# Two batch normalisations: powers of two for both in one set, epsilon and pivot scalars on GpSimd, the weights' mean copied by ScalarE

## The chip, the cores and the metric

The kernel runs on one core of a Trainium2 chip. The metric is the device time of one execution in microseconds (us), as the median of several runs. A core has TensorE (PE for matmuls, PEld for weight loads), VectorE (DVE), ScalarE (ACT), GpSimd (POOL) and SyncE (SP), each with an instruction queue of its own; they meet through semaphores.

## The reference

The input is 8 images of 64 channels and 16 x 16 pixels. Four layers follow each other; the change lies in the third and at the joint with the fourth.

```python
# layers 0 and 1: self attention over the 256 pixels of each image, with a shortcut
# layer 2
def batch_norm(x, gamma, beta):
    mean = jnp.mean(x, axis=(0, 2, 3), keepdims=True)
    var = jnp.mean((x - mean) ** 2, axis=(0, 2, 3), keepdims=True)
    return (x - mean) * rsqrt(var + 1e-5) * gamma[None, :, None, None] + beta[None, :, None, None]
def quantize_w1bit(w):
    return jnp.mean(jnp.abs(w)) * jnp.sign(w)
out = relu(batch_norm(x, gamma0, beta0))
out = conv3x3(out, quantize_w1bit(w0))
out = relu(batch_norm(out, gamma1, beta1))
out = conv3x3(out, quantize_w1bit(w1)) + x
# layer 3: whitening of groups of 4 channels: means, 4x4 covariance, Cholesky, solve, 4x4 weights, bias
```

## The kernel before

The 128 partitions hold two halves of the batch (G = 2) with 64 channels each; the free dimension holds four pairs of images (PAIRS, written q = 0 to 3) of 256 pixels. Everything is written out by hand: each engine has one list of instructions, and its order is the order of the code. The stages are: attention layers 0 and 1 (eight iterations of `project`, `scores`, `values`, `mix`), batch normalisation and convolution 0, batch normalisation and convolution 1, and the whitening.

A convolution is 9 taps on a high and a low part of the input (`hi` and `lo`, 16 bit numbers whose sum is the 32 bit activation). `conv_steps` (line 924) issues 41 steps on TensorE: first images 0 and 2, beside them and five steps later images 1 and 3. Image 2's high part is due at step 18, image 3's at 23, image 2's low part at 27 and image 3's at 32. The weights of a tap are the sign of the weight times a power of two (`tap_values`, line 427, on GpSimd); the factor E, the mean of the absolute weights, is left out of convolution 0 and made good in the epsilon of the second normalisation: its statistics get epsilon / E² added.

`power_of_two(n)` (line 1038) makes, from gamma and beta of normalisation n, the power of two near their maximum and the scaled gamma and beta: five VectorE instructions, each of which waits for the one before (`step`). It stands for n = 0 first of all VectorE's work (line 1117), and for n = 1 amid convolution 0 (line 1232).

Between the inputs of convolution 0 and the statistics of its outputs VectorE has this list (lines 1222 to 1242): the low parts of images 0 and 1 (`first_low`); a copy of the weights' means out of PSUM (`emean`); two instructions for E² and its floor (`esq`); high and low part of image 2 (`later_inputs`); the reciprocal `einv`; high and low part of image 3; `power_of_two(1)`; the statistics of image 0 (`conv0_statistics`); epsilon times the reciprocal, and its addition to the statistics (`eps1`, semaphore `eps1_set`); statistics of image 1; the two pivot scalars `nscale` and `nxm` (semaphore `pivot_set`); statistics of images 2 and 3.

TensorE, after convolution 0, waits for `eps1_set` and for three statistics, adds up the two halves of the batch for images 0 to 2 (`combine(1, range(3))`, line 975), then waits for the fourth statistics and does the rest (line 977). VectorE's `bn_aggr` (line 1211) waits for that; the second normalisation and convolution 1 hang on it. The first normalisation has the same sequence in lines 957 to 962 and 1175; ahead of its last statistics VectorE copies the whitening weights (line 1172, semaphore `w3_set`). GpSimd, in this time, does the tap values of convolution 0, the scale and shift of normalisation 0 (lines 447 to 454), the tap values of convolution 1 (line 456), and the scale and shift of normalisation 1. `keep_warm` issues matmuls on constants whose result is not used.

Of the kernel before, what the change touches and what calls it, by code (L numbers as in the profile page):

```python
# [17 lines left out]
U32 = mybir.dt.uint32  # L18
ALU = mybir.AluOpType
# [3 lines left out]
P = 128  # L23
# [3 lines left out]
N = H * W  # L27
# [23 lines left out]
WARM_START = (6, 5, 4)  # L51
E_SQUARE_MIN = 1e-37
FP16_ROOM = 128.0
# [8 lines left out]
K_ID = 0  # L62
K_MH = K_ID + P
K_FIRST = K_MH + 1
K_AVG = K_FIRST
# [15 lines left out]
def constants():  # L81

    part = np.arange(P)
    same_c = part[:, None] % C == part[None, :] % C
    same_g = part[:, None] // C == part[None, :] // C
    k = np.zeros((P, K_COLS), np.float32)
    k[:, K_ID:K_ID + P] = np.eye(P)
    k[:, K_AVG:K_AVG + P] = 0.5 * same_c
    k[:, K_DIF:K_DIF + P] = np.where(same_c, np.where(same_g, 0.5, -0.5), 0)
    k[:, K_REP:K_REP + P] = (part[:, None] % CJ == part[None, :] % CJ) / NTOT  # L90
    k[:, K_ONES:K_ONES + P] = 1.0 / (P * C * TAPS)
    k[:, K_MASKJ:K_MASKJ + C] = part[:, None] % CJ == part[None, :C] % CJ
    k[:, K_HOT:K_HOT + Q] = (part[:, None] % C) // CJ == np.arange(Q)
    k[:, K_EXPO] = -0.5
    k[:, K_EXPO + 1:K_EXPO + Q] = -0.5 * k[:, K_HOT + 1:K_HOT + Q]
    k[:, K_EPSN:K_EPSN + Q * Q] = (BN_EPS * NTOT / G * k[:, K_HOT:K_HOT + Q, None]
                                   * np.eye(Q)).reshape(P, Q * Q)
    k[:, K_MH] = -0.5
    for g in range(G):
        k[:, K_OWN + g * P:K_OWN + (g + 1) * P] = same_c * (part[:, None] // C == g)  # L100
    return k
# [16 lines left out]
def build(nc, x, attn_w, params, consts, select, conv_w, out):  # L118
    with ExitStack() as ctx:
        def sb(name, shape, dt=F32):  # L120
            return ctx.enter_context(nc.sbuf_tensor(name, shape, dt))
# [35 lines left out]
        bn_b = [sb(f"bn_b{n}", [P, 1]) for n in range(2)]  # L157
        bn_t = [sb(f"bn_t{n}", [P, 8]) for n in range(2)]

        sign = [sb(f"sign{n}", [P, TAPS, C]) for n in range(2)]  # L160
        taps = [sb(f"taps{n}", [P, TAPS, C], BF16) for n in range(2)]
        wabs = [sb(f"wabs{n}", [P, 1]) for n in range(2)]
        esq, einv, eps1 = (sb(name, [P, 1]) for name in ("esq", "einv", "eps1"))
        emean = sb("emean", [P, 2])
# [76 lines left out]
        sign_out, taps_out = sem("sign_out"), sem("taps_out")  # L241
        wabs_out, e_mm = sem("wabs_out"), sem("e_mm")
        bn_v, pivot_set = sem("bn_v"), sem("pivot_set")
        tap_mm, tap_sum_out = sem("tap_mm"), sem("tap_sum_out")
# [108 lines left out]
        def _(pool):  # L353
# [73 lines left out]
            def tap_values(n):  # L427

                pool.wait_ge(sign_out, n + 1)
                pool.wait_ge(pow2_out, n + 1)  # L430
                nc.gpsimd.tensor_scalar(taps[n][:], sign[n][:], bn_t[n][:, 2:3], 1.0,
                                        ALU.mult, ALU.mult).then_inc(taps_out, 1)
                pool.wait_ge(taps_out, n + 1)
# [9 lines left out]
            pool.wait_ge(shift_out, 8)  # L443
            tap_values(0)
            for n in range(2):

                pool.wait_ge(var_out, n + 1)
                pool.wait_ge(rstd_out, n + 1)
                nc.gpsimd.tensor_tensor(bn_s[n][:], bn_t[n][:, 4:5], rstd[n][:], ALU.mult).then_inc(scale_out, 1)
                pool.wait_ge(scale_out, n + 1)  # L450
                nc.gpsimd.tensor_tensor(bn_b[n][:], mv[n][:, 0:1], bn_s[n][:], ALU.mult).then_inc(shift_part, 1)
                pool.wait_ge(shift_part, n + 1)
                nc.gpsimd.tensor_tensor(bn_b[n][:], bn_t[n][:, 5:6], bn_b[n][:], ALU.subtract).then_inc(shift0_set, 1)
                pool.wait_ge(shift0_set, n + 1)
                if n == 0:
                    tap_values(1)
            pool.wait_ge(pre_out, 1)
# [20 lines left out]
        def _(act):  # L478
# [117 lines left out]
            for n in range(2):  # L596
# [8 lines left out]
                for q in range(2):  # L605

                    act.wait_ge(z_out, 2 * n + q + 1)
                    out_hi = hi[n][:, q].rearrange("p r w -> p (r w)")
                    if n == 1 and q == 1:
                        nc.scalar.activation(out_hi, zn[n][:, q], ACT.Relu, scale=rstd[n][:], bias=bn_t[n][:, 5:6],  # L610
                                             accum_out=act_sum[:]).then_inc(hi_act, 1)
                    else:
                        nc.scalar.activation(out_hi, zn[n][:, q], ACT.Relu, scale=rstd[n][:],  # L613
                                             bias=bn_t[n][:, 5:6]).then_inc(hi_act, 1)
                act.wait_ge(shift0_set, n + 1)
                for q in range(2, PAIRS):
                    if n == 1:

                        act.wait_ge(lo_out, q + 1)
                    src = xs[LAYERS][:, quarter(q)] if n == 0 else pb_conv[0][q][:, 0:N]  # L620
                    nc.scalar.activation(act32[:, quarter(q)], src, ACT.Relu, scale=bn_s[n][:],
                                         bias=bn_b[n][:]).then_inc(act_out, 1)

            act.wait_ge(pivot_mm, 1)
# [401 lines left out]
        def _(dve):  # L1026
# [10 lines left out]

            def power_of_two(n):

                t, col = bn_t[n], (P_BNG0, P_BNG1)[n]  # L1040
                step(ve.tensor_reduce(t[:, 0:1], prm[:, col:col + 2], AX.X, ALU.max, apply_absolute_value=True))
                step(ve.tensor_scalar(t[:, 1:2], t[:, 0:1], 1e-30, 1.0 / FP16_ROOM, ALU.max, ALU.mult))
                step(ve.tensor_scalar(t[:, 2:3].bitcast(U32), t[:, 1:2].bitcast(U32), 0x7F800000, None,
                                      ALU.bitwise_and))
                ve.reciprocal(t[:, 3:4], t[:, 2:3]).then_inc(pow2_out, 1)
                dve.wait_ge(pow2_out, n + 1)
                step(ve.tensor_scalar(t[:, 4:6], prm[:, col:col + 2], t[:, 3:4], None, ALU.mult))

# [57 lines left out]
            def statistics(b):  # L1106
# [4 lines left out]
                if b == 0:  # L1111
# [4 lines left out]

            power_of_two(0)
            first_parts(0)
# [47 lines left out]
            statistics(1)  # L1166
            weight_sum(1)
            values_out(7)
            add_shortcut(6)
            statistics(2)  # L1170

            ve.tensor_copy(tt[:, :, Q:2 * Q],
                           prm[:, P_W3:P_W3 + Q * Q].rearrange("p (i r) -> p i r", i=Q)).then_inc(w3_set, 1)
            dve.wait_ge(pv_mm, ITERS)
# [9 lines left out]
            def first_line(n, q):  # L1184

                ve.tensor_scalar(act32[:, quarter(q)], zn[n][:, q], rstd[n][:], bn_t[n][:, 5:6],  # L1186
                                 ALU.mult, ALU.add).then_inc(line_out, 1)
# [21 lines left out]
            for n in range(2):  # L1209
                dve.wait_ge(comb_mm, n + 1)  # L1210
                ve.bn_aggr(mv[n][:], both[:, :, 0:GROUPS]).then_inc(var_out, 1)  # L1211
                dve.wait_ge(var_out, n + 1)
                t = bn_t[n]
                for q in range(2):
                    src = xs[LAYERS][:, quarter(q)] if n == 0 else pb_conv[0][q][:, 0:N]
                    ve.tensor_scalar(zn[n][:, q], src, mv[n][:, 0:1], t[:, 4:5], ALU.subtract,  # L1216
                                     ALU.mult).then_inc(z_out, 1)
# [3 lines left out]
                if n == 0:  # L1221
                    first_line(0, 1)
                    first_low(0, 0)
                    first_low(0, 1)
                    dve.wait_ge(e_mm, 1)
                    step(ve.tensor_copy(emean[:], pb_mean[:, 0:2]))
                    step(ve.tensor_tensor(esq[:], emean[:, 0:1], emean[:, 0:1], ALU.mult))
                    step(ve.tensor_scalar(esq[:], esq[:], E_SQUARE_MIN, None, ALU.max))
                    later_inputs(0, 2)
                    step(ve.reciprocal(einv[:], esq[:]))  # L1230
                    later_inputs(0, 3)
                    power_of_two(1)
                    conv0_statistics(0)
                    step(ve.tensor_scalar(eps1[:], einv[:], BN_EPS * PAIRS * N, None, ALU.mult))
                    dve.wait_ge(stats_out, 1)
                    ve.tensor_tensor(stats[1][:, M2:M2 + 1], stats[1][:, M2:M2 + 1], eps1[:],
                                     ALU.add).then_inc(eps1_set, 1)
                    conv0_statistics(1)
                    ve.tensor_scalar(nscale[:], emean[:, 1:2], -1.0 / N, None, ALU.mult).then_inc(pivot_set, 1)
                    ve.tensor_scalar(nxm[:], mv[0][:, 0:1], -1.0, None, ALU.mult).then_inc(pivot_set, 1)  # L1240
                    conv0_statistics(2)
                    conv0_statistics(3)
                else:
# [3 lines left out]
                    for q in range(2, PAIRS):  # L1247
                        later_inputs(1, q)
            for q in range(PAIRS):
                dve.wait_ge(conv_mm, PAIRS + q + 1)  # L1250
# [132 lines left out]
```

## Time and profile before

| | |
|---|---|
| time, median of 3 runs | 68.54 us (68.48 to 69.81) |
| span of the profiled execution, first to last instruction | 68.0 us |
| median less span, taken as what lies around the span | 0.54 us |
| busy: PE, VectorE, ScalarE, GpSimd | 87%, 70%, 63%, 29% |
| granted TensorE clock, mean | 0.999 |

No time of the profiled execution itself is recorded beside its span, so the median stands for it. In the rows below, a time is microseconds from the start of the span; a duration is that of the instruction, and the next one of the same engine can start before it is over. "xN" puts N like instructions that follow each other in one row. In brackets stands how long the engine was idle before, and what ended the wait; "issue" means that the profile shows nothing it waited for.

### The profile page before, as it was taken

To read this page: it belongs to the slowest core of one execution; us is meant where nothing else is said; L and a number is where in the kernel's file an instruction comes from. 1 tells how busy PE (TensorE), PEld (TensorE's weight loads), DVE (VectorE), ACT (ScalarE), POOL (GpSimd) and SP (SyncE) were. 2 spreads that over 40 slices of the span, in tenths; PEclk is the share of its full clock that TensorE was granted. 3 is DMA by queue.
4 is the path that set the end of the run, shared out by engine and by line. 5 is a ranking of instruction groups with operands and counts; after the bars stand their busy time and mean duration, and the time that the engine had idled before them with its cause. 6 is when DMAs were issued, how large, how long until landed. Compare 5 with 4: busy or idle time off the path is not lost. (4 is left out here: it accounts for less than half of the span.)

```text
span 68.0 us, 2165 instructions
## 1 busy us (share of the span) xinstructions
PE 59.0 (87%) x811; PEld 36.5 (54%) x811; DVE 47.9 (70%) x133; ACT 42.5 (63%) x137; POOL 20.0 (29%) x58
## 2 busy tenths in 40 slices
PE   5969999888989998995999897999769999999910
PEld 3315354446655554652436384598655997955500
DVE  0077569878694989997693856998979978576530
ACT  0710229899999599969999495670018573267630
POOL 5000770733083632766032104200403050036000
PEclk9999999999999999999999999999999999999999
DMA  0878940000000000000000000000000000000044
GB/s 0 236 219 222 339 195 0 0 0 10 0 0 0 5 0 0 0 10 10 0 0 0 0 10 0 0 0 10 0 0 0 10 0 10 0 0 0 0 162 146
DMA packets 2457, 2.71 MB, mean 40 GB/s; under 512 B 400, under 2 KB 2064, under 8 KB 2448
## 3 DMA queue, kind: packets, MB, share of 16 engines
q1 hardware_dynamic: 2160, 2.39, 11.3%
q10 hardware_dynamic: 288, 0.20, 0.9%
q8 instruction: 6, 0.10, 0.6%
q14 instruction: 3, 0.02, 0.1%
HBM read 2.06 MB, written 0.52 MB: 38 GB/s over the span
## 5 line engine op out<-in xcount | busy, mean ns | idle before, releaser
L686 PE MATMUL bank<-const-bfloat16-1.0 128*64 128x512 bf16 x64 | 9.2, 429 | 0.8 <-PEq L1368 0.8
L530 ACT ACTIVATE probs<-bank 128x512 f32<-128x512 f32 x16 | 8.8, 601 | 1.1 <-PE bank L769 1.1
L510 ACT ACTIVATE bank<-bank,negmax 128x256 f32<-128x256 f32 x20 | 9.1, 460 | 0.2 <-DVE negmax L1060 0.2
L808 PE MATMUL both<-probs,vt 128*64 128x256 f32 x56 | 7.6, 387 | 0.3 <-issue 0.3
L1060 DVE TENSOR_REDUCE negmax<-bank 128x2 f32<-128x512 f32 x10 | 6.7, 685 | 1.4 <-PE bank L745 0.8
L510 ACT ACTIVATE both<-both,negmax 128x256 f32<-128x256 f32 x12 | 5.4, 451 | 2.6 <-DVE negmax L1060 2.6
L363 POOL TENSOR_TENSOR cut<-cut 64x256 f32<-64x256 f32 x7 | 4.3, 611 | 8.7 <-DVE cut L1070 5.7
L916 PE MATMUL bank<-hi,taps 64*64 64x225 f16 (+2 forms) x126 | 6.3, 267 | 0.1
L916 PE MATMUL bank<-lo,taps 64*64 64x225 f16 (+2 forms) x126 | 6.2, 266 | 0.0
L686 PEld LDWEIGHTS bank<-const-bfloat16-1.0 128*64 128x64 bf16 x64 | 3.7, 119 | 3.7 <-issue 1.6
L916 PEld LDWEIGHTS bank<-hi,taps 64*64 64x64 bf16 x126 | 5.2, 107 | 0.8 <-issue 0.4
L916 PEld LDWEIGHTS bank<-lo,taps 64*64 64x64 bf16 x126 | 5.6, 107 | 0.0
L1087 DVE CAST qk<-bank 128x512 bf16<-128x512 f32 x7 | 4.8, 683 | 0.5 <-PE bank L713 0.5
L379 POOL TENSOR_TENSOR shift<-negmax,lntot 128x4 f32<-128x4 f32 x8 | 1.6, 203 | 11.9 <-issue 10.5
L808 PEld LDWEIGHTS both<-probs,vt 128*64 128x64 f32 x56 | 4.4, 136 | 1.4 <-issue 0.8
L1060 DVE TENSOR_REDUCE negmax<-both 128x2 f32<-128x512 f32 x6 | 4.1, 683 | 1.1 <-PE bank L745 1.1
L697 PE MATMUL both<-x,aw 128*64 128x256 f32 x24 | 4.8, 484 | 0.1
L370 POOL TENSOR_TENSOR cut<-cut 32x256 f32<-32x256 f32 x7 | 4.3, 611 | 0.5
L510 ACT ACTIVATION_READ_ACCUMULATOR bank<-bank,negmax 128x1 f32 x20 | 4.4, 219 | 0.0
L1093 DVE COPY vt<-bank 128x256 f32<-128x256 f32 x8 | 3.4, 421 | 1.4 <-PE bank L729 1.4
L713 PE MATMUL bank<-cut,half 128*64 128x256 bf16 x32 | 3.8, 315 | 0.3 <-POOL cut L370 0.2
L538 ACT ACTIVATE shift_t<-bank 128x256 bf16<-128x256 f32 x8 | 3.1, 385 | 1.3 <-PE bank L784 1.2
(155 smaller groups left out, 124.8 us busy)
## 6 DMA issues: line engine op xcount, KB each, us to landing
cw<-conv_w SPq DMA_DIRECT2D x2, 288.0 KB, 4.4
x<-x_in SPq DMA_DIRECT2D x4, 128.0 KB, 3.1
out<-res SPq DMA_DIRECT2D x4, 128.0 KB, 1.8
kst<-consts SPq DMA_DIRECT2D x1, 428.0 KB, 5.0
aw<-attn_w ACTq DMA_DIRECT2D x1, 128.0 KB, 2.5
aw<-attn_w SPq DMA_DIRECT2D x1, 128.0 KB, 2.9
half<-select SPq DMA_DIRECT2D x1, 96.0 KB, 3.3
kst<-consts SPq DMA_DIRECT2D x1, 64.5 KB, 4.0
```

Source lines behind the costliest of these rows:

```text
L363: nc.gpsimd.tensor_tensor(some, some, tops(some), ALU.subtract).then_inc(part1_out, 1)
L370: nc.gpsimd.tensor_tensor(some, some, tops(some), ALU.subtract).then_inc(part2_out, 1)
L510: nc.scalar.activation(part, part, ACT.Exp, bias=negmax[:, i % 2, n:n + 1], accum_out=total[:, i % 2, n:n + 1]).then_inc(total_out, 1)
L530: nc.scalar.activation(probs[:, i % 2, g], pb_t[g][:].rearrange("p (t n) -> p t n", t=CH), ACT.Exp).then_inc(exp_out, 1)
L686: mm(bank[lanes(h)], filler[:, lanes(h)], filled, start=True, stop=True)
L697: last = mm(proj(i)[lanes(h)], aw[:, w + h * C:w + (h + 1) * C], x_of(i), start=True, stop=True)
L713: last = mm(to, half[:, 1 + o, lanes(h)], tops(cut[:, i]), start=True, stop=True)
L808: last = mm(mixed(i)[g * C:(g + 1) * C], vt[:, i % 2, t, g * C:(g + 1) * C], probs[:, i % 2, g, t, :], start=(t == 0 and i < ITERS - 1), s ...
L916: last = mm(img(pb_conv[n][q][lanes(to), 0:N])[:, kept(dy, H), kept(dx, W)], taps[n][lanes(g), tap, :], (hi, lo)[part][n][lanes(g), q, shi ...
L1060: ve.tensor_reduce(negmax[:, i % 2, g * CH:(g + 1) * CH], pb_s[(2 * i + g) % 3][:].rearrange("p (t n) -> p t n", t=CH), AX.X, ALU.max, neg ...
L1087: ve.tensor_copy(qk[:, i].rearrange("p o n -> p (o n)"), pb_rep[:]).then_inc(qk_out, 1)
L1093: ve.tensor_copy(vt[:, i % 2], pb_v[:, 0:CH * P].rearrange("p (t c) -> p t c", t=CH)).then_inc(v_out, 1)
```

## The change

- The two sets of five VectorE instructions become one set for both normalisations at the start of the kernel, with twice as many numbers in each. Its last instruction is a `tensor_tensor` with a repeated operand in place of a `tensor_scalar`.
- The copy of the weights' means goes to ScalarE, behind its two last activations for convolution 0. VectorE waits for it (`emean_out`) before the residual of convolution 1.
- The floor, 1 / E², epsilon and its addition to the statistics, and the two pivot scalars go to GpSimd (`epsilon`), behind the scale and shift of normalisation 0. The square and the reciprocal become one power (`ALU.pow` with the exponent -2 from a column of the constants that held another number).
- GpSimd makes the tap values of convolution 1 directly behind those of convolution 0.
- VectorE copies the whitening weights ahead of the last `values_out` rather than ahead of the last statistics.

```diff
-K_MH = K_ID + P
+K_M2 = K_ID + P
...
-    k[:, K_MH] = -0.5
+    k[:, K_M2] = -2.0
...
-                pool.wait_ge(pow2_out, n + 1)
-                nc.gpsimd.tensor_scalar(taps[n][:], sign[n][:], bn_t[n][:, 2:3], 1.0,
+                pool.wait_ge(pow2_out, 1)
+                nc.gpsimd.tensor_scalar(taps[n][:], sign[n][:], pow2[:, n:n + 1], 1.0,
...
             tap_values(0)
+            tap_values(1)
+
+            def epsilon():
+
+                pool.wait_ge(emean_out, 1)
+                nc.gpsimd.tensor_scalar(e_floor[:], emean[:, 0:1], E_MIN, 1.0, ALU.max, ALU.mult).then_inc(floor_out, 1)
+                pool.wait_ge(floor_out, 1)
+                nc.gpsimd.tensor_tensor(einv[:], e_floor[:], kst[:, K_M2:K_M2 + 1], ALU.pow).then_inc(einv_out, 1)
+                pool.wait_ge(einv_out, 1)
+                nc.gpsimd.tensor_scalar(eps1[:], einv[:], BN_EPS * PAIRS * N, 1.0, ALU.mult, ALU.mult).then_inc(eps_out, 1)
+                pool.wait_ge(eps_out, 1)
+                pool.wait_ge(stats_out, 1)
+                nc.gpsimd.tensor_tensor(stats[1][:, M2:M2 + 1], stats[1][:, M2:M2 + 1], eps1[:],
+                                        ALU.add).then_inc(eps1_set, 1)
+                nc.gpsimd.tensor_scalar(nscale[:], emean[:, 1:2], -1.0 / N, 1.0, ALU.mult, ALU.mult).then_inc(pivot_set, 1)
+                nc.gpsimd.tensor_scalar(nxm[:], mv[0][:, 0:1], -1.0, 1.0, ALU.mult, ALU.mult).then_inc(pivot_set, 1)
+                pool.wait_ge(eps1_set, 1)
+                pool.wait_ge(pivot_set, 2)
+
             for n in range(2):
...
-                nc.gpsimd.tensor_tensor(bn_s[n][:], bn_t[n][:, 4:5], rstd[n][:], ALU.mult).then_inc(scale_out, 1)
+                nc.gpsimd.tensor_tensor(bn_s[n][:], gb[:, n, 0:1], rstd[n][:], ALU.mult).then_inc(scale_out, 1)
...
                 if n == 0:
-                    tap_values(1)
+                    epsilon()
...
+                if n == 0:
+                    act.wait_ge(e_mm, 1)
+                    nc.scalar.activation(emean[:], pb_mean[:, 0:2], ACT.Identity).then_inc(emean_out, 1)
...
-            def power_of_two(n):
-
-                t, col = bn_t[n], (P_BNG0, P_BNG1)[n]
-                step(ve.tensor_reduce(t[:, 0:1], prm[:, col:col + 2], AX.X, ALU.max, apply_absolute_value=True))
-                step(ve.tensor_scalar(t[:, 1:2], t[:, 0:1], 1e-30, 1.0 / FP16_ROOM, ALU.max, ALU.mult))
-                step(ve.tensor_scalar(t[:, 2:3].bitcast(U32), t[:, 1:2].bitcast(U32), 0x7F800000, None,
+            def powers_of_two():
+
+                both_gb = prm[:, P_BNG0:P_BNG0 + 4].rearrange("p (n k) -> p n k", n=2)
+                step(ve.tensor_reduce(gb_max[:], both_gb, AX.X, ALU.max, apply_absolute_value=True))
+                step(ve.tensor_scalar(gb_room[:], gb_max[:], 1e-30, 1.0 / FP16_ROOM, ALU.max, ALU.mult))
+                step(ve.tensor_scalar(pow2[:].bitcast(U32), gb_room[:].bitcast(U32), 0x7F800000, None,
                                       ALU.bitwise_and))
-                ve.reciprocal(t[:, 3:4], t[:, 2:3]).then_inc(pow2_out, 1)
-                dve.wait_ge(pow2_out, n + 1)
-                step(ve.tensor_scalar(t[:, 4:6], prm[:, col:col + 2], t[:, 3:4], None, ALU.mult))
+                ve.reciprocal(ipow2[:], pow2[:]).then_inc(pow2_out, 1)
+                dve.wait_ge(pow2_out, 1)
+                step(ve.tensor_tensor(gb[:], both_gb, ipow2[:].unsqueeze(2).to_broadcast([P, 2, 2]), ALU.mult))
...
             weight_sum(1)
+            ve.tensor_copy(tt[:, :, Q:2 * Q],
+                           prm[:, P_W3:P_W3 + Q * Q].rearrange("p (i r) -> p i r", i=Q)).then_inc(w3_set, 1)
             values_out(7)
             add_shortcut(6)
             statistics(2)
 
-            ve.tensor_copy(tt[:, :, Q:2 * Q],
-                           prm[:, P_W3:P_W3 + Q * Q].rearrange("p (i r) -> p i r", i=Q)).then_inc(w3_set, 1)
             dve.wait_ge(pv_mm, ITERS)
...
                     first_low(0, 1)
-                    dve.wait_ge(e_mm, 1)
-                    step(ve.tensor_copy(emean[:], pb_mean[:, 0:2]))
-                    step(ve.tensor_tensor(esq[:], emean[:, 0:1], emean[:, 0:1], ALU.mult))
-                    step(ve.tensor_scalar(esq[:], esq[:], E_SQUARE_MIN, None, ALU.max))
                     later_inputs(0, 2)
-                    step(ve.reciprocal(einv[:], esq[:]))
                     later_inputs(0, 3)
-                    power_of_two(1)
-                    conv0_statistics(0)
-                    step(ve.tensor_scalar(eps1[:], einv[:], BN_EPS * PAIRS * N, None, ALU.mult))
-                    dve.wait_ge(stats_out, 1)
-                    ve.tensor_tensor(stats[1][:, M2:M2 + 1], stats[1][:, M2:M2 + 1], eps1[:],
-                                     ALU.add).then_inc(eps1_set, 1)
-                    conv0_statistics(1)
-                    ve.tensor_scalar(nscale[:], emean[:, 1:2], -1.0 / N, None, ALU.mult).then_inc(pivot_set, 1)
-                    ve.tensor_scalar(nxm[:], mv[0][:, 0:1], -1.0, None, ALU.mult).then_inc(pivot_set, 1)
-                    conv0_statistics(2)
-                    conv0_statistics(3)
+                    for q in range(PAIRS):
+                        conv0_statistics(q)
...
+            dve.wait_ge(emean_out, 1)
             for q in range(PAIRS):
                 dve.wait_ge(conv_mm, PAIRS + q + 1)
```

The other lines of the diff give new names to the same tiles.

## Rows read from the trace of the kernel before

**Rows 1.** The page: busy tenths of 40 slices of the span

```profile
PE   5969999888989998995999897999769999999910
DVE  0077569878694989997693856998979978576530
PEclk9999999999999999999999999999999999999999
```

**Rows 2.** Chain that ended last, 40 to 42.6: start, length, what

```profile
41.46 0.20 DVE tt L1172
41.65 0.33 DVE stats L1175
...
42.49 0.39 DVE mv L1211
```

**Rows 3.** Chain that ended last, 48 to 50.9

```profile
49.35 0.35 DVE stats L1207
...
49.84 0.58 PE both L892 x16
...
50.44 0.39 DVE mv L1211
```

**Rows 4.** VectorE in order of time, 45 to 50.1

```profile
45.09 0.14 DVE L1226 COPY emean<-bank 128x2 f32<-128x2 f32 x1
...
45.65 0.29 DVE L1199 CAST hi<-act 128x256 f16<-128x256 f32 x1
45.98 0.43 DVE L1201 TENSOR_TENSOR lo<-act,hi 128x256 f16<-128x256 f32 x1
46.32 0.16 DVE L1230 RECIPROCAL einv<-esq 128x1 f32<-128x1 f32 x1
...
47.18 0.15 DVE L1041 TENSOR_REDUCE bn_t<-prm 128x1 f32<-128x2 f32 x1
...
49.27 0.75 DVE L1207 BATCH_NORM_STATS2 stats<-bank 128x6 f32<-128x256 f32 x2
```

**Rows 5.** TensorE's matmuls and weight loads in order of time, convolution 0

```profile
42.80 1.49 PE L686 MATMUL bank<-const-bfloat16-1.0 128*64 128x512 bf16 x12
44.22 1.18 PE L916 MATMUL bank<-hi,taps 64*64 64x256 f16 x30
...
46.86 0.35 PEld L916 LDWEIGHTS bank<-hi,taps 64*64 64x64 bf16 x13 [0.20 <-DVE hi L1199]
...
47.73 1.21 PE L916 MATMUL bank<-lo,taps 64*64 64x240 f16 x25
```

**Rows 6.** VectorE in order of time, the start and 38.5 to 39.7

```profile
4.28 0.23 DVE L1047 TENSOR_SCALAR bn_t<-prm,bn_t 128x2 f32<-128x2 f32 x1
4.68 0.48 DVE L1070 TENSOR_SCALAR cut<-both,prm 128x256 f32<-128x256 f32 x1 [0.17 <-PE both L697]
...
38.55 0.73 DVE L1052 TENSOR_REDUCE wabs<-cw 128x1 f32<-128x576 f32 x1
39.60 0.42 DVE L1093 COPY vt<-bank 128x256 f32<-128x256 f32 x1 [0.33 <-PE bank L729]
```

**Rows 7.** GpSimd in order of time

```profile
40.88 0.75 POOL L431 TENSOR_SCALAR taps<-sign,bn_t 128x576 bf16<-128x576 f32 x1 [3.14 <-issue]
43.57 0.19 POOL L449 TENSOR_TENSOR bn_s<-bn_t,rstd 128x1 f32<-128x1 f32 x1 [1.95 <-ACT rstd L603]
43.84 0.19 POOL L451 TENSOR_TENSOR bn_b<-mv,bn_s 128x1 f32<-128x1 f32 x1
...
60.51 1.83 POOL L467 TENSOR_TENSOR roots<-tt,kst 128x1 f32<-128x1 f32 x3 [4.68 <-DVE tt L1278]
```

**Rows 8.** The instructions of line 467: ns least/median/most, first and last start

```profile
L467 POOL TENSOR_TENSOR roots<-tt,kst x3: 553/556/564, 60.5 to 61.8; 128x1 f32<-128x1 f32 x3
```

**Rows 9.** ScalarE in order of time

```profile
44.43 1.08 ACT L621 ACTIVATE act<-x,bn_b,bn_s 128x256 f32<-128x256 f32 x2
54.38 0.35 ACT L626 ACTIVATE npre<-bank,nxm,nscale 128x1 f32<-128x1 f32 x1 [0.79 <-PE bank L992]
```

More of the change, by code:

```diff
@@ L51 @@
 WARM_START = (6, 5, 4)
-E_SQUARE_MIN = 1e-37
+E_MIN = 3.2e-19
 FP16_ROOM = 128.0
@@ L62 @@
 K_ID = 0
-K_MH = K_ID + P
-K_FIRST = K_MH + 1
+K_M2 = K_ID + P
+K_FIRST = K_M2 + 1
 K_AVG = K_FIRST
@@ L157, in build @@
         bn_b = [sb(f"bn_b{n}", [P, 1]) for n in range(2)]
-        bn_t = [sb(f"bn_t{n}", [P, 8]) for n in range(2)]
+        gb_max, gb_room, pow2, ipow2 = (sb(name, [P, 2]) for name in ("gb_max", "gb_room", "pow2", "ipow2"))
+        gb = sb("gb", [P, 2, 2])
         sign = [sb(f"sign{n}", [P, TAPS, C]) for n in range(2)]
@@ L162, in build @@
         wabs = [sb(f"wabs{n}", [P, 1]) for n in range(2)]
-        esq, einv, eps1 = (sb(name, [P, 1]) for name in ("esq", "einv", "eps1"))
+        e_floor, einv, eps1 = (sb(name, [P, 1]) for name in ("e_floor", "einv", "eps1"))
         emean = sb("emean", [P, 2])
@@ L242, in build @@
         wabs_out, e_mm = sem("wabs_out"), sem("e_mm")
+        emean_out, floor_out, einv_out, eps_out = (sem("emean_out"), sem("floor_out"), sem("einv_out"),
+                                                   sem("eps_out"))
         bn_v, pivot_set = sem("bn_v"), sem("pivot_set")
@@ L452, in _ @@
                 pool.wait_ge(shift_part, n + 1)
-                nc.gpsimd.tensor_tensor(bn_b[n][:], bn_t[n][:, 5:6], bn_b[n][:], ALU.subtract).then_inc(shift0_set, 1)
+                nc.gpsimd.tensor_tensor(bn_b[n][:], gb[:, n, 1:2], bn_b[n][:], ALU.subtract).then_inc(shift0_set, 1)
                 pool.wait_ge(shift0_set, n + 1)
                 if n == 0:
-                    tap_values(1)
+                    epsilon()
             pool.wait_ge(pre_out, 1)
@@ L609, in _ @@
                     if n == 1 and q == 1:
-                        nc.scalar.activation(out_hi, zn[n][:, q], ACT.Relu, scale=rstd[n][:], bias=bn_t[n][:, 5:6],
+                        nc.scalar.activation(out_hi, zn[n][:, q], ACT.Relu, scale=rstd[n][:], bias=gb[:, n, 1:2],
                                              accum_out=act_sum[:]).then_inc(hi_act, 1)
@@ L613, in _ @@
                         nc.scalar.activation(out_hi, zn[n][:, q], ACT.Relu, scale=rstd[n][:],
-                                             bias=bn_t[n][:, 5:6]).then_inc(hi_act, 1)
+                                             bias=gb[:, n, 1:2]).then_inc(hi_act, 1)
                 act.wait_ge(shift0_set, n + 1)
@@ L1114, in statistics @@
                                      ALU.add).then_inc(stats0_out, 1)
-            power_of_two(0)
+            powers_of_two()
             first_parts(0)
@@ L1184, in first_line @@
             def first_line(n, q):
-                ve.tensor_scalar(act32[:, quarter(q)], zn[n][:, q], rstd[n][:], bn_t[n][:, 5:6],
+                ve.tensor_scalar(act32[:, quarter(q)], zn[n][:, q], rstd[n][:], gb[:, n, 1:2],
                                  ALU.mult, ALU.add).then_inc(line_out, 1)
@@ L1212, in _ @@
                 dve.wait_ge(var_out, n + 1)
-                t = bn_t[n]
                 for q in range(2):
                     src = xs[LAYERS][:, quarter(q)] if n == 0 else pb_conv[0][q][:, 0:N]
-                    ve.tensor_scalar(zn[n][:, q], src, mv[n][:, 0:1], t[:, 4:5], ALU.subtract,
+                    ve.tensor_scalar(zn[n][:, q], src, mv[n][:, 0:1], gb[:, n, 0:1], ALU.subtract,
                                      ALU.mult).then_inc(z_out, 1)
```

## The prediction

> **What bounds the kernel now.** I read the page's slices first [rows 1]. TensorE is busy nearly throughout, but much of that is filler, and it has one dip in the 29th and 30th slice (each is 1.7 us), while VectorE is full there; the granted clock is at its upper level (2.4 GHz) all along, so no clock step enters the sum. The chain of waits then says which engine ends last in each stage. Up to the last statistics of normalisation 0 it is attention's tail, with VectorE's weight copy between two statistics [rows 2]. From there to the second `bn_aggr` it is VectorE: statistics, then TensorE's 16 `combine` matmuls, then `bn_aggr` [rows 3]. VectorE in order of time shows why: the little instructions that the change moves stand between the large ones [rows 4]. TensorE in order of time shows what convolution 0 itself needs: it starts at 44.22, stands still once, for 0.20 us, for image 3's high part, and ends at 47.73 + 1.21 = 48.94 [rows 5]. The second `bn_aggr` starts at 50.44, 1.50 us later [rows 3]. Behind it, TensorE's own list (filler, convolution 1, transposes, Gram matrix, filler) follows as a whole, so what `bn_aggr` gains, the end gains.
>
> **What is taken off VectorE.** Between 45.09 and 47.18 stand 2.09 us; two pairs of cast and `lo` stay, each 46.32 - 45.65 = 0.67 us from start to start, so 0.75 goes (`emean`, two `esq`, `einv`). Between 47.18 and the last two statistics at 49.27 stand again 2.09; two statistics stay, each worth 0.35 in the chain [rows 3], so 1.39 goes (the five power instructions, two for epsilon, two pivot scalars) [rows 4]. Together 2.14 us. That isn't the gain, since TensorE's convolution is next late.
>
> **Term 1, the weight copy.** It fills 0.20 us of the chain ahead of the last statistics [rows 2]. Without it these can start 0.20 sooner if the last `mix` is ready; the profile names no wait there, so I bound the gain by 0 and 0.20 and take 0.20, as the statistics of the images before followed their data directly. In its new place it follows the weight sum, which ends at 38.55 + 0.73 = 39.28; VectorE then waited until 39.60 for TensorE [rows 6]. The gap of 0.32 covers 0.20; without that cover it would cost 0.20. Everything up to the start of convolution 0 moves along, the filler in front of it too, which TensorE issues behind `combine` [rows 5]: start 44.02.
>
> **Term 2, the stall in convolution 0.** Net of the stall it took 48.94 - 44.22 - 0.20 = 4.52 us for 41 steps, 0.11 each [rows 5]. VectorE is now at image 2 at 45.09 - 0.20 = 44.89 instead of 45.65, and with steps of 0.33 and 0.34 [rows 4] high and low part of image 2 are done at about 45.2 and 45.65, those of image 3 at 45.85 and 46.32. They are due at steps 18, 27, 23 and 32, so at 46.0, 47.0, 46.55 and 47.55: 0.7 us to spare or more. ScalarE's input for image 3 ends at 44.43 + 1.08 - 0.20 = 45.31 [rows 9], before VectorE's cast of it at 45.56. The stall goes, 0.20, and the convolution ends at 44.02 + 4.52 = 48.54.
>
> **Term 3, the statistics.** Those of images 0 and 1 come while the convolution runs, those of image 2 when step 35 is done, about 48.1. The last ones start 0.04 behind the convolution's end (49.84 + 0.58 = 50.42 to 50.44 is such a hand-over [rows 3]) and take 0.42 (two with a pitch of 0.33 to 0.35 take 0.75 [rows 4]): 49.00. From the end of the last statistics to `bn_aggr` it was 42.49 - 41.98 = 0.51 at normalisation 0 [rows 2], and 0.42 at the other, where the chain ran through image 2's statistics and all 16 matmuls in one go (end of the last statistics 49.27 + 0.75 = 50.02) [rows 3, 4]. As image 2 now is half a microsecond ahead, the case is that of normalisation 0: `bn_aggr` at 49.51. The lag behind the convolution shrinks from 1.50 to 0.97, so 0.53 (0.62 by the shorter hand-over). The sum is 0.20 + 0.20 + 0.53 = 0.93 us.
>
> **What GpSimd and ScalarE get.** ScalarE copies the means behind its two inputs, at 45.31; a copy of two columns isn't in the trace on this engine, so I take the longest small one, 0.35 [rows 9], and 0.1 for the hand-over: GpSimd begins at 45.76, long past its scale and shift (which start 0.2 earlier than 43.57). Its small instructions follow each other at 43.84 - 43.57 = 0.27 [rows 7], the powers at 1.83 / 3 = 0.61, and I allow 0.64. Floor 46.03, power 46.67, product 46.94, addition (the statistics of image 0 are in by then) 47.13. TensorE asks for `eps1_set` only with image 2's statistics, at 48.7. So 1.57 us cover this chain; without the cover every further tenth is a tenth of the time. Bounds: 0.19 and 0.61 for each of the four instructions put the chain's end between 46.7 and 48.3, still hidden. The pivot scalars follow by 47.7 and ScalarE wants them at 54.38 - 0.93 = 53.45 [rows 9]. The tap values of convolution 1 now stand ahead of normalisation 0's scale: GpSimd has them from 40.88 + 0.75 = 41.63 to 42.38, and the scale waits for 43.57 - 0.20 anyway [rows 7]; queued behind is only that scale and shift. VectorE's new wait for `emean_out` lies 9 us after the copy.
>
> **At the start** the five instructions take twice the numbers, from two columns to four. VectorE was idle 0.17 us behind them, waiting for TensorE's first projection [rows 6]. The added elements are few, the bounds for the five together are -0.06 and +0.2, and the idle time hides all but 0.03: nothing.
>
> So the profiled execution's span of 68.0 becomes 67.07; it lies 0.54 under the median, which I take to stay outside the span: 68.54 - 0.93 = 67.61, say 67.6.
>
> **The rivals.**
>
> GpSimd holds VectorE up: 67.9. Its six new instructions (five at 0.19, one at 0.56 [rows 7, 8]: 1.51 us) now run while VectorE casts and subtracts, where before GpSimd had nothing. If VectorE stood still for all of it, image 3's low part would come at 46.32 + 1.51 = 47.83, against 47.55 due: 0.28 lost, 0.65 gained. For it: no row of before has GpSimd beside these instructions. Against: they must meet exactly, and four of the six run after 46.3, when VectorE has only statistics out of PSUM left.
> The Trainium skill, page "SBUF — State Buffer", section "Who interferes with whom", states that a VectorE instruction with two SBUF inputs or in a 2-port mode and a GpSimd instruction that reads SBUF exclude each other for the length of one. The case above is that rule at its worst, and no row of before can test it.
>
> The copy pays nothing: 67.8. If the last `mix` and not the weight copy held the last statistics, term 1 is 0; and if the gap at 39.3 doesn't cover it, the sum falls to 0.53 and the time to 68.0. For it: bounds only; against: the chain goes through the copy.
>
> GpSimd's first power is slow, and the kernel gets slower: 70.6. The power now is this program's first, 14 us earlier than before. Before, GpSimd sat idle for 4.68 us ahead of its first power [rows 7]; anything done once for a first use could have been hidden in there. If 4.68 us fell due here, `eps1_set` would come at 47.13 + 4.68 = 51.81 and `combine` about 0.1 later, at 51.9 instead of 49.84 [rows 3]: 2.07 us on top of 68.54. It decides from 49.74 - 47.13 = 2.6 us on; from 1.57 on it eats the gain. Against: the three powers took 553 to 564 ns, the first no longer than the others [rows 8], and nothing shows a preparation.
> The Trainium skill, page "GPSIMD Engine Reference", section "2.1 Instruction dispatch", puts the first call of a newly loaded GpSimd function at about 6 us more, without an instruction in the profile. An estimate by that page is 47.13 + 6 = 53.1, so about 71.9; the trace shows no such wait in front of the first power, but it can't see behind the idle time.
>
> **How the numbers follow.** Forecast 67.6: 0.77. VectorE held up, 67.9: 0.09. Copy without use, 67.8 to 68.0: 0.06. More than I see, under 67.17: 0.04. Slow first power, 70.6: 0.04. The range of 8 in 10 has the shorter hand-over and some measuring spread below, 67.2, and the two weak cases above, 68.1. Two per cent of 68.54 are 1.37 us, about what a measurement of this kernel can tell from no change; a gain of 0.93 (1.4%) lies inside. Faster by over 2%: 0.06; within 2%: 0.90; slower by over 2%: 0.04.
>
> **What would show it.** In the changed profile: the last statistics of attention start directly behind those of image 2, and convolution 0 near 44.0 (term 1); no wait for `hi` in it, end near 48.55 (term 2); the last statistics within 0.1 of that end and `bn_aggr` near 49.5 (term 3); GpSimd's addition near 47.1, well before image 2's statistics, and a power of 0.56. Wrong it would be if TensorE waited for GpSimd in front of `combine`, if the cast or `lo` rows stretched beyond 0.29 and 0.43 beside GpSimd, or if attention shifted by more than a tenth.

## The result: 1.7% faster, and the profile after

The changed kernel takes 0.9834 of the time of the kernel before (95% interval 0.9815 to 0.9853), which is 1.14 us of 68.45 where 0.93 were forecast: 67.17 to 67.38 us against 68.41 to 68.54. Some executions, of either kernel, spend some 1.4 to 1.5 us more in their start-up; times and ratios leave them out, but the profiles behind the rows of before and behind two experiments are such, so times in a profile are counted from a common point, the second last shortcut addition (the last one on VectorE), which is at 40.51 before and at 39.03 after.

VectorE of the changed kernel in order of time, at the start and then from the weight copy to the second `bn_aggr`:

```profile
4.15 0.16 DVE L1072 TENSOR_TENSOR gb<-prm,ipow 128x4 f32<-128x4 f32 x1
4.52 0.48 DVE L1095 TENSOR_SCALAR cut<-both,prm 128x256 f32<-128x256 f32 x1 [0.20 <-PE both L722]
...
37.72 0.17 DVE L1193 COPY tt<-prm 128x16 f32<-128x16 f32 x1
38.13 0.42 DVE L1118 COPY vt<-bank 128x256 f32<-128x256 f32 x1 [0.24 <-PE bank L754]
39.03 0.48 DVE L1128 SCALAR_TENSOR_TENSOR x<-both,prm,x 128x256 f32<-128x256 f32 x1 [0.48 <-PE both L833]
...
40.84 0.38 DVE L1236 BATCH_NORM_AGGREGATE mv<-both 128x2 f32<-128x48 f32 x1 [0.52 <-PE both L917]
...
43.44 0.28 DVE L1224 CAST hi<-act 128x256 f16<-128x256 f32 x1
43.75 0.43 DVE L1226 TENSOR_TENSOR lo<-act,hi 128x256 f16<-128x256 f32 x1
44.09 0.31 DVE L1224 CAST hi<-act 128x256 f16<-128x256 f32 x1
44.44 0.42 DVE L1226 TENSOR_TENSOR lo<-act,hi 128x256 f16<-128x256 f32 x1
44.78 0.88 DVE L1232 BATCH_NORM_STATS2 stats<-bank 128x6 f32<-128x256 f32 x2
46.58 0.79 DVE L1232 BATCH_NORM_STATS2 stats<-bank 128x6 f32<-128x256 f32 x2 [0.92 <-PE bank L941]
47.79 0.38 DVE L1236 BATCH_NORM_AGGREGATE mv<-both 128x2 f32<-128x48 f32 x1 [0.42 <-PE both L917]
```

The casts follow `lo` at once, and the statistics come in two pairs with 0.92 us of waiting for TensorE between them, where before VectorE waited nowhere [rows 4]. TensorE of the changed kernel (convolution 0 and the `combine` behind it):

```profile
42.57 1.18 PE L941 MATMUL bank<-hi,taps 64*64 64x256 f16 x30
...
45.74 1.15 PE L941 MATMUL bank<-lo,taps 64*64 64x225 f16 x30
47.16 0.56 PE L917 MATMUL both<-stats,kst 64*64 64x18 f32 x16 [0.26 <-DVE stats L1232]
```

Convolution 0 now lasts 45.74 + 1.15 - 42.57 = 4.32 us, with no wait for `hi` in it; it lasted 4.72 [rows 5]. GpSimd of the changed kernel:

```profile
44.08 0.37 POOL L453 TENSOR_SCALAR e_floor<-emean 128x1 f32<-128x1 f32 x1 [1.43 <-ACT emean L647]
44.52 0.76 POOL L455 TENSOR_TENSOR einv<-e_floor,kst 128x1 f32<-128x1 f32 x1
...
45.65 0.19 POOL L460 TENSOR_TENSOR stats<-stats,eps 128x1 f32<-128x1 f32 x1
```

Its chain ends at 45.84, and TensorE's `combine` could start with image 2's statistics, which end at 46.58 + 0.44 = 47.02 (one such instruction takes 0.43 to 0.44): 1.18 us to spare. The floor and the power took 0.18 and 0.20 longer than a small instruction and a power did before [rows 7, 8]; both began beside a cast or a subtraction of VectorE.

From the common point to the second `bn_aggr` it is 47.79 - 39.03 = 8.76 us; before it was 50.44 - 40.51 = 9.93. The difference, 1.17, is the whole gain within the interval.

### The profile page after: what moved, and what is told of

Same layout as the page of the kernel before. It is cut to its first block and busy times, and to the rows that moved or that the text cites. A ratio compares the mean times of both kernels' runs of the same rounds, so it can differ in the third digit from the quotient of the medians.

```text
span 65.4 us, 2158 instructions
## 1 busy us (share of the span) xinstructions
PE 56.9 (87%) x811; PEld 35.6 (54%) x811; DVE 46.2 (71%) x120; ACT 42.5 (65%) x138; POOL 21.8 (33%) x64
## 3 DMA queue, kind: packets, MB, share of 16 engines
HBM read 2.06 MB, written 0.52 MB: 39 GB/s over the span
## 5 line engine op out<-in xcount | busy, mean ns | idle before, releaser
L722 PE MATMUL both<-x,aw 128*64 128x256 f32 x24 | 4.3, 440 | 0.1
```

Of the source, the lines that this page charges most:

```text
L722: last = mm(proj(i)[lanes(h)], aw[:, w + h * C:w + (h + 1) * C], x_of(i), start=True, stop=True)
```

## Experiments

Ratios are to the kernel before, with 95% intervals; the changed kernel's is 0.9834. "Span A" is the time from the second last shortcut addition to the second `bn_aggr` in the profile, 8.76 in the changed kernel; it doesn't contain the start-up.

**The kernel before, once more.** No edit.

> The kernel before once more, unchanged, for a profile whose start-up can be laid beside that of the changed kernel. In the profile shown ahead of the prediction TensorE's projections of the first images took 1.06 to 1.12 us each, in the changed kernel's the later ones 0.6. If that is a matter of the single run, this one has the third add of the shortcut of layer 1 near 39.0 instead of 40.5 and a span near 66.6; if the new start of VectorE's list brought it, it stays near 40.5.

68.3 us, span 66.5. VectorE and TensorE of this run in order of time:

```profile
39.02 0.48 DVE L1103 SCALAR_TENSOR_TENSOR x<-both,prm,x 128x256 f32<-128x256 f32 x1 [0.48 <-PE both L808]
...
41.01 0.38 DVE L1211 BATCH_NORM_AGGREGATE mv<-both 128x2 f32<-128x48 f32 x1 [0.52 <-PE both L892]
...
42.73 0.40 PE L916 MATMUL bank<-hi,taps 64*64 64x256 f16 x4
...
46.24 1.21 PE L916 MATMUL bank<-lo,taps 64*64 64x240 f16 x25
...
48.95 0.38 DVE L1211 BATCH_NORM_AGGREGATE mv<-both 128x2 f32<-128x48 f32 x1 [0.42 <-PE both L892]
```

The addition is at 39.02, as in the changed kernel: the new start of VectorE's list did not move it. Span A is 9.93, the same as in the rows of before, and convolution 0 lasts 46.24 + 1.21 - 42.73 = 4.72 again. Laid side by side, the changed kernel is 0.17 to 0.18 ahead at the first `bn_aggr`, 0.56 at the end of convolution 0 and 1.16 at the second `bn_aggr`.

**The weight copy back in its place.**

```diff
             weight_sum(1)
-            ve.tensor_copy(tt[:, :, Q:2 * Q],
-                           prm[:, P_W3:P_W3 + Q * Q].rearrange("p (i r) -> p i r", i=Q)).then_inc(w3_set, 1)
             values_out(7)
...
+            ve.tensor_copy(tt[:, :, Q:2 * Q],
+                           prm[:, P_W3:P_W3 + Q * Q].rearrange("p (i r) -> p i r", i=Q)).then_inc(w3_set, 1)
             dve.wait_ge(pv_mm, ITERS)
```

> The changed kernel with the copy of the whitening weights back ahead of the last statistics. Theory (the copy lies on the path): 0.17 us slower than the changed kernel, and the last statistics 0.2 behind those of image 2. Rival (the last mix sets them): no difference.

Ratio 0.9868 (0.9845 to 0.9890), 0.23 us above the changed kernel's, with overlapping intervals. The profile is sharper:

```profile
39.27 0.48 DVE L1128 SCALAR_TENSOR_TENSOR x<-both,prm,x 128x256 f32<-128x256 f32 x1 [0.48 <-PE both L833]
...
41.25 0.38 DVE L1236 BATCH_NORM_AGGREGATE mv<-both 128x2 f32<-128x48 f32 x1 [0.52 <-PE both L917]
...
48.20 0.38 DVE L1236 BATCH_NORM_AGGREGATE mv<-both 128x2 f32<-128x48 f32 x1 [0.42 <-PE both L917]
```

Span A is 8.93, 0.17 more, and all of it ahead of the first `bn_aggr` (1.98 against 1.81). The copy was on the path.

**The powers of two of normalisation 1 back amid convolution 0,** and with them the tap values of convolution 1 behind epsilon.

```diff
-            powers_of_two()
+            power_of_two(0)
             first_parts(0)
...
                     later_inputs(0, 3)
+                    power_of_two(1)
                     for q in range(PAIRS):
                         conv0_statistics(q)
...
             tap_values(0)
-            tap_values(1)
...
                     epsilon()
+                    tap_values(1)
```

> The changed kernel with the powers of two of normalisation 1 back in their old place amid convolution 0, and the tap values of convolution 1 behind epsilon. Theory (TensorE's convolution is next late, not VectorE's list): the 1.0 us of power instructions lie in VectorE's 0.92 us of waiting ahead of image 2's statistics and end as these are due, so 0 to 0.1 us slower than the changed kernel. Rival (each microsecond taken off VectorE is a microsecond of the time): 1.0 us slower.

Ratio 0.9839 (0.9818 to 0.9860): no difference. VectorE:

```profile
39.15 0.48 DVE L1128 SCALAR_TENSOR_TENSOR x<-both,prm,x 128x256 f32<-128x256 f32 x1 [0.48 <-PE both L833]
...
44.53 0.42 DVE L1226 TENSOR_TENSOR lo<-act,hi 128x256 f16<-128x256 f32 x1
...
45.90 1.59 DVE L1232 BATCH_NORM_STATS2 stats<-bank 128x6 f32<-128x256 f32 x4
47.91 0.38 DVE L1236 BATCH_NORM_AGGREGATE mv<-both 128x2 f32<-128x48 f32 x1 [0.42 <-PE both L917]
```

The power instructions fill the time between `lo` and 45.90, and the four statistics follow each other with no wait, just in time. Span A is 8.76, to the hundredth that of the changed kernel. A whole microsecond of VectorE's list is worth nothing by itself; the theory that a microsecond off VectorE is one off the time is out.

**Means, epsilon and pivot scalars back on VectorE.**

```diff
                     first_low(0, 1)
+                    dve.wait_ge(e_mm, 1)
+                    step(ve.tensor_copy(emean[:], pb_mean[:, 0:2]))
+                    step(ve.tensor_tensor(esq[:], emean[:, 0:1], emean[:, 0:1], ALU.mult))
+                    step(ve.tensor_scalar(esq[:], esq[:], E_SQUARE_MIN, None, ALU.max))
                     later_inputs(0, 2)
+                    step(ve.reciprocal(einv[:], esq[:]))
                     later_inputs(0, 3)
...
-                    epsilon()
...
-                    nc.scalar.activation(emean[:], pb_mean[:, 0:2], ACT.Identity).then_inc(emean_out, 1)
```

and epsilon and pivots between the statistics, as before.

> The changed kernel with the copy of the means, epsilon and the pivot scalars back on VectorE in their old places; the powers stay at the start. Theory: 0.75 us of them stand ahead of image 3's high part, so convolution 0 stalls again and lasts 4.72 instead of 4.32: 0.40 us slower than the changed kernel; the other 0.38 us are covered by the wait for image 2. Rival (the list counts): 1.1 us slower. Rival (moving work to GpSimd cost as much as it gave): no difference.

Ratio 0.9876 (0.9849 to 0.9903), 0.29 us above the changed kernel's, with intervals that overlap a little; the profile is again sharper. VectorE, TensorE's matmuls and one row of its weight loads:

```profile
40.55 0.48 DVE L1106 SCALAR_TENSOR_TENSOR x<-both,prm,x 128x256 f32<-128x256 f32 x1 [0.48 <-PE both L811]
...
44.08 1.19 PE L919 MATMUL bank<-hi,taps 64*64 64x256 f16 x30
...
46.72 0.35 PEld L919 LDWEIGHTS bank<-hi,taps 64*64 64x64 bf16 x13 [0.20 <-DVE hi L1202]
...
47.59 1.21 PE L919 MATMUL bank<-lo,taps 64*64 64x240 f16 x25
...
48.23 0.43 DVE L1210 BATCH_NORM_STATS2 stats<-bank 128x6 f32<-128x256 f32 x1
48.84 0.43 DVE L1210 BATCH_NORM_STATS2 stats<-bank 128x6 f32<-128x256 f32 x1 [0.18 <-PE bank L919]
49.69 0.38 DVE L1214 BATCH_NORM_AGGREGATE mv<-both 128x2 f32<-128x48 f32 x1 [0.42 <-PE both L895]
```

Image 3's high part is late again (the wait of 0.20), convolution 0 lasts 47.59 + 1.21 - 44.08 = 4.72, and span A is 9.14: 0.38 more. The last statistics still wait 0.18 for TensorE, so the lag behind the convolution is that of the changed kernel (49.69 - 48.80 = 0.89, there 0.90). Epsilon's instructions cost through the stall alone.

**One and four more powers on GpSimd.** In `epsilon`, k = 1 and k = 4, results unused:

```diff
                 pool.wait_ge(floor_out, 1)
+                for k in range(4):
+                    nc.gpsimd.tensor_tensor(spare[:, k:k + 1], e_floor[:], kst[:, K_M2:K_M2 + 1], ALU.pow)
                 nc.gpsimd.tensor_tensor(einv[:], e_floor[:], kst[:, K_M2:K_M2 + 1], ALU.pow).then_inc(einv_out, 1)
```

> The changed kernel with one more power instruction on GpSimd between the floor and the power of epsilon, its result unused. Theory: the chain ends some 0.6 us later, at 46.4 to 46.5, still ahead of image 2's statistics at 47.02: no difference. Rival (GpSimd's instructions hold VectorE up by their length): 0.2 us or more slower.

Ratio 0.9835 (0.9821 to 0.9850): no difference. In its profile:

```profile
39.19 0.48 DVE L1131 SCALAR_TENSOR_TENSOR x<-both,prm,x 128x256 f32<-128x256 f32 x1 [0.48 <-PE both L836]
...
46.30 0.19 POOL L463 TENSOR_TENSOR stats<-stats,eps 128x1 f32<-128x1 f32 x1
...
47.94 0.38 DVE L1239 BATCH_NORM_AGGREGATE mv<-both 128x2 f32<-128x48 f32 x1 [0.42 <-PE both L920]
```

> The same with four more powers. Theory: the chain ends 2.2 to 2.6 us later, at 48.0 to 48.4, and TensorE's combine, which started at 47.16, waits for it: 1.0 to 1.4 us slower than the changed kernel, slightly slower than the kernel before or level with it. If the cover were larger than the 1.2 us read from the trace, less.

Ratio 0.9924 (0.9909 to 0.9939), 0.62 us above the changed kernel's: less than the 1.0 to 1.4 expected. TensorE, GpSimd and VectorE:

```profile
39.10 0.48 DVE L1131 SCALAR_TENSOR_TENSOR x<-both,prm,x 128x256 f32<-128x256 f32 x1 [0.48 <-PE both L836]
...
47.78 0.19 POOL L463 TENSOR_TENSOR stats<-stats,eps 128x1 f32<-128x1 f32 x1
...
48.02 0.41 PE L920 MATMUL both<-stats,kst 64*64 64x18 f32 x16 [1.06 <-POOL stats L463]
...
48.51 0.38 DVE L1239 BATCH_NORM_AGGREGATE mv<-both 128x2 f32<-128x48 f32 x1 [1.07 <-PE both L920]
```

Now TensorE waits for GpSimd in front of `combine`. With one power more the chain ended 0.49 later (taken from the common point) and cost nothing; with four, 2.06 later. Of these 1.18 are cover; the 16 matmuls then run in one go in 0.41 instead of 0.56, as all statistics are there, and follow the release by 0.05 instead of 0.14: 2.06 - 1.18 - 0.24 = 0.64, and span A is 9.41, 0.65 more. The cover read from the trace was right. The expectation missed two things: the four powers put the chain off by 2.06 and not by 2.2 to 2.6, and a late `eps1_set` makes `combine` itself shorter.

**The tap values of convolution 1 beside the casts.**

```diff
             tap_values(0)
-            tap_values(1)
...
                 pool.wait_ge(emean_out, 1)
+                tap_values(1)
```

> The changed kernel with the tap values of convolution 1 (0.75 us of GpSimd) right behind the copy of the means, beside VectorE's casts and subtractions for images 2 and 3. In the changed kernel's trace GpSimd's floor and power took 0.2 us longer than a like instruction alone when they met these. Theory: GpSimd waits, VectorE's cast and subtraction stay within 0.03 of 0.28 and 0.43, and the chain ends about 0.8 to 1.0 later, inside its cover of 1.2: no difference. Rival (VectorE waits as long as GpSimd's instruction lasts): image 3's low part up to 0.75 late, still 0.3 ahead of its step, so the time hardly moves but the rows stretch.

Ratio 0.9812 (0.9787 to 0.9838): no difference. GpSimd and VectorE in order of time:

```profile
40.42 0.48 DVE L1128 SCALAR_TENSOR_TENSOR x<-both,prm,x 128x256 f32<-128x256 f32 x1 [0.48 <-PE both L833]
...
45.46 0.85 POOL L434 TENSOR_SCALAR taps<-sign,pow 128x576 bf16<-128x576 f32 x1 [1.42 <-ACT emean L647]
45.48 0.30 DVE L1224 CAST hi<-act 128x256 f16<-128x256 f32 x1
45.81 0.77 DVE L1226 TENSOR_TENSOR lo<-act,hi 128x256 f16<-128x256 f32 x1
...
46.75 0.56 POOL L455 TENSOR_TENSOR einv<-e_floor,kst 128x1 f32<-128x1 f32 x1
...
49.17 0.38 DVE L1236 BATCH_NORM_AGGREGATE mv<-both 128x2 f32<-128x48 f32 x1 [0.42 <-PE both L917]
```

Half of the expectation fell: not only GpSimd waited. VectorE's subtraction took 0.77 instead of 0.43; it ended at 46.58, 0.27 after GpSimd's instruction at 46.31. The cast, which by the trace also began behind GpSimd's instruction, was not held up (0.30). The power, which now starts behind that subtraction, takes 0.56. It cost nothing (span A 8.75): without the hold image 3's low part is ready 1.1 us ahead of its step (32 steps of 0.105 from 42.57 in the changed kernel are 45.93, its end 44.86), of which the hold took 0.34.

**Fewer fillers.**

```diff
-WARM = (4, 6, 2, 4, 1, 15)
+WARM = (4, 5, 2, 4, 1, 14)
```

> The changed kernel with one filler less ahead of convolution 0 (5 instead of 6 pairs) and one less ahead of the final matmuls (14 instead of 15 pairs). The first convolution's input is ready at 42.43, and TensorE starts it at 42.57, behind the fillers: 0.13 us sooner. The final weights are ready 0.2 before the last filler ends: up to 0.15 sooner. Together 0.13 to 0.25 us faster than the changed kernel if the granted clock stays at its upper level.

Ratio 0.9814 (0.9799 to 0.9828), 0.14 us below the changed kernel's, with overlapping intervals; against the kernel with one more power, measured together with it and no slower than the changed kernel, it is the same 0.14. TensorE and VectorE of this kernel, and behind them the last row of TensorE in the changed kernel:

```profile
39.05 0.48 DVE L1128 SCALAR_TENSOR_TENSOR x<-both,prm,x 128x256 f32<-128x256 f32 x1 [0.48 <-PE both L833]
...
42.54 0.60 PE L941 MATMUL bank<-hi,taps 64*64 64x256 f16 x8
...
45.72 1.19 PE L941 MATMUL bank<-lo,taps 64*64 64x225 f16 x29
...
47.80 0.38 DVE L1236 BATCH_NORM_AGGREGATE mv<-both 128x2 f32<-128x48 f32 x1 [0.42 <-PE both L917]
...
61.70 0.45 PE L1046 MATMUL bank<-zc,final_w 64*64 64x128 f32 x8 [0.16 <-DVE res L1325]
```

```profile
61.80 0.45 PE L1046 MATMUL bank<-zc,final_w 64*64 64x128 f32 x8 [0.15 <-DVE res L1325]
```

The filler ahead of convolution 0 gave nothing: the convolution starts 0.05 sooner and ends no sooner (45.72 + 1.19 = 46.91, span A 8.75). The one ahead of the final matmuls gave some 0.12: from the common point to the last row of them it is 61.70 - 39.05 = 22.65 us, in the changed kernel 61.80 - 39.03 = 22.77. The granted clock was 1.00 in every run of this kernel. This is the fastest version that was run; that it beats the kernel before is clear, that it beats the changed kernel rests on one trace of each.

## Why the prediction was right, and where its sizes were off

The sign, the mechanism and the place were right: of some 2.1 us taken off VectorE about 1.0 came back, because TensorE's convolution is next late; the weight copy gave 0.17 more, and nothing behind the second `bn_aggr` took the gain up again. The forecast of 0.93 is 0.24 short of the 1.17 between the common point and `bn_aggr`, and term 2 is most of that.

Term 1, the weight copy: 0.20 forecast, 0.17 to 0.18 measured, shown alone by its undoing. The gap in front of `values_out` covered it: 0.24 of waiting is left.

Term 2, the stall: 0.20 forecast, 0.39 to 0.40 measured. This is the term most in error. "It stands still once, for 0.20 us" was read off the weight loads' idle time [rows 5] and taken for the whole loss, and from it came the 0.11 us of a step. An undisturbed convolution lasts 4.32 us for 41 steps, 0.105 each. The row showed only how long the queue stood for image 3's high part, and that is half of what the late images cost. That the whole 0.40 goes with them is shown by the kernel with epsilon back on VectorE, where that wait of 0.20 returns and the convolution lasts 4.72 again. Where the other half goes is not shown; I would look for it in steps that one of the two interleaved chains of images does without the other.

Term 3, the lag of the statistics: 0.53 forecast, 0.60 measured (1.50 to 0.90). The step "the case is that of normalisation 0" failed: the hand-over from the last statistics to `bn_aggr` was 0.42, as in normalisation 1 before, not 0.51. How far image 2 is ahead doesn't decide it. In the kernel with epsilon back on VectorE image 2's statistics start 0.61 ahead of the last ones (48.23 and 48.84), more than the half microsecond that was assumed, and the hand-over is 0.42 all the same (49.27 to 49.69). What normalisation 0 has more stands in its chain before, ahead of `bn_aggr` at 42.49 [rows 2]:

```profile
42.03 0.34 PE both L892 x8
...
42.40 0.05 DVEq L1210
```

DVEq is VectorE's own queue of instructions: the wait for `combine` (line 1210) is an instruction of its own there. Its 0.05 and the 0.04 behind it make the 0.09; in normalisation 1 no such piece stands between `combine` and `bn_aggr` [rows 3].

The parts don't add up edit by edit. Powers back: 0.00. Epsilon back: 0.38. Both back, with the copy: 1.17 less 0.17, so 1.00. The lag of 0.60 is paid only if both stand in VectorE's list, because TensorE's convolution leaves VectorE room for either.

GpSimd's chain had 1.18 us of cover where 1.57 were worked out. Taken from the common point, its deadline came 0.20 sooner than forecast, as the convolution was that much quicker, and its end 0.19 later: floor and power stretched by 0.38 together, and ScalarE's copy of the means gave 0.20 back, with 0.15 instead of the bound of 0.35. The bounds of that chain, 46.7 and 48.3, are 46.5 and 48.2 by the prediction's own figures; nothing hung on it. The start was as said: the last power instruction ends at 4.31, and VectorE waits 0.20 for the projection, 0.17 before [rows 6].

The rivals: GpSimd did hold VectorE up when one of its long instructions was put in the way (0.34 us), but in the changed kernel itself the second cast took 0.31 where the first took 0.28, and that was all. The copy did pay. A slow first power didn't come: it took 0.76. The 0.20 above its usual 0.56 belong to VectorE's subtraction beside it, not to a first use: with the tap values beside the casts the power, again the program's first, came behind the subtraction and took 0.56. The Trainium skill ("GPSIMD Engine Reference", "2.1 Instruction dispatch") puts the first call of a freshly loaded function at about 6 us more; no such time stands in front of the first power here, which starts 0.07 behind the floor.

The 0.54 us taken as lying around the span was wrong too, without harm to the difference: it is 68.3 - 66.5 = 1.8 and 67.17 - 65.4 = 1.8. The first reading of the slices was loose as well: TensorE also dips in the 19th and the 25th slice (5 and 7 tenths), and VectorE has 9 and 7 tenths in the 29th and 30th [rows 1]. No term of the sum comes from there.

## What to carry to other kernels

Before counting what an engine is relieved of, find the next one that the stage waits for: here 1.0 us of one edit was worth nothing alone, and 0.6 with the other edit undone as well. When two streams are interleaved in one queue, the idle time in front of a late input need not be all that it costs (0.20 of 0.40 here); compare with a stretch of the same work that never waited. And before small dependent work moves to an idle engine, work out its deadline: the cover was 1.2 us here, and adding to the chain tested it.

## What the runs showed of the hardware

GpSimd and VectorE held each other up in SBUF. A GpSimd instruction of 128 x 576 that began at 45.46, 0.35 ahead of a two-input subtraction in SBUF, held the subtraction up: 0.77 us instead of 0.43, its end 0.27 behind GpSimd's. A cast that began 0.02 behind the same instruction was not held up (0.30), and GpSimd's instruction took 0.85 instead of 0.75. The other way round, a small GpSimd instruction that met a subtraction and a cast took 0.37 instead of 0.19, and a power that began while a subtraction ran took 0.76 instead of 0.56; beside statistics out of PSUM the power took 0.56.

The Trainium skill ("SBUF — State Buffer", "Who interferes with whom") says that a VectorE instruction with two SBUF inputs, or in a 2-port mode, and a GpSimd instruction that reads SBUF share a pair of ports, and that whoever issues first has it for its whole instruction. The trace agrees for the subtraction, which ends behind GpSimd's instruction, and for the power. For the cast it fits if the cast ran outside a 2-port mode or came first, and no run here shows which. The stretch was more than I expected for instructions of one column.
